# Masked cross attention of a two-layer decoder: how heads, softmax sums and stacked operands travel through memory

## The reference

```python
def _L0_xattn_ref(target, source, target_mask, source_mask, Wq, bq, Wk, bk, Wv, bv):
    # SIZE = 256, HEADS = 16, HEAD_DIM = 16, NEG = 1e6; target = x and source = ctx, (b, 256, 512)
    q = jnp.einsum('oc,bct->bot', Wq, target) + bq[None, :, None]
    k = jnp.einsum('oc,bcs->bos', Wk, source) + bk[None, :, None]
    v = jnp.einsum('oc,bcs->bos', Wv, source) + bv[None, :, None]
    ...
    dot = jnp.einsum('bhdt,bhds->bhts', q, k) / math.sqrt(HEAD_DIM)
    mask = target_mask[:, :, :, None] * source_mask[:, :, None, :]
    dot = mask * dot - (1.0 - mask) * NEG
    amap = jax.nn.softmax(dot, axis=-1) * mask
    out = jnp.einsum('bhts,bhds->bhdt', amap, v)
    return out.reshape(b, HEADS * HEAD_DIM, t)
...
x = _layernorm(x + _L0_xattn_ref(x, ctx, mask, mask, Wq, bq, Wk, bk, Wv, bv))
```

## Time and profile before

| | |
|---|---|
| Three timed runs | 3818.95, 3791.48, 3818.0 us; median 3818.0 |
| The profiled execution, its own time | 3803.1 us |
| Its span, first to last instruction | 3801.3 us |
| The changed stage, in the span | about 453 to 1309 us |
| Busy over the whole span | PE 82%, DVE 44%, ACT 33%, POOL 14% |
| Mean granted TensorE clock | 0.909 of full speed |

### The profile page before, as it was taken

The page is one execution under the profiler, slowest core; times in us unless marked ns, Lnnn a source line. Parts: engine busy times, 40 slices in busy tenths (PEclk is TensorE's granted clock), DMA queues, the critical chain, the costliest instruction groups (busy, mean ns, idle before and its releaser), DMA issues. The chain is left out here.

```text
span 3801.3 us, 48719 instructions
## 1 busy us (share of the span) xinstructions
PE 3109.5 (82%) x16306; PEld 2055.6 (54%) x16339; DVE 1682.5 (44%) x3232; ACT 1257.8 (33%) x3220; POOL 546.1 (14%) x551
## 2 busy tenths in 40 slices
PE   6999647786766469999978888599999997799894
PEld 5666422222222157777755555488888886444441
DVE  5666534554545222211215666366666665211113
ACT  2333214444444311111104444355565553111110
POOL 1000200111110120000000000233333332300002
PEclk9999867877888689999989999799999998999997
DMA  1000174434444220000010000211121113500323
GB/s 67 12 22 22 53 133 81 93 79 87 92 93 72 68 82 23 12 12 12 12 47 12 22 22 17 100 40 45 46 81 63 45 33 114 226 0 33 121 88 108
DMA packets 123827, 227.30 MB, mean 60 GB/s; under 512 B 14392, under 2 KB 27192, under 8 KB 123664
## 3 DMA queue, kind: packets, MB, share of 16 engines
q1 hardware_dynamic: 107488, 186.54, 18.3%
q0 software_dynamic: 7664, 27.40, 2.1%
q10 hardware_dynamic: 8512, 11.20, 1.0%
HBM read 157.36 MB, written 63.01 MB: 58 GB/s over the span
## 5 line engine op out<-in xcount | busy, mean ns | idle before, releaser
L1261 DVE TENSOR_REDUCE x_minus_max<-banks 128x2 f32<-128x1024 f32 x256 | 308.8, 1220 | 266.7 <-PE banks L1325 261.4
L1206 ACT ACTIVATE x_probs<-banks 128x512 f32<-128x512 f32 x512 | 285.9, 595 | 283.6 <-PE banks L1343 223.4
L1343 PE MATMUL banks<-x_stacked_q,x_stacked_k 53*128 53x512 f32 x512 | 254.7, 560 | 106.0 <-ACT x_probs L1206 70.0
L1325 PE MATMUL banks<-x_stacked_k,x_stacked_q 51*128 51x512 f32 x512 | 204.1, 529 | 106.2 <-DVE x_minus_max L1261 79.4
L1343 PEld LDWEIGHTS banks<-x_stacked_q,x_stacked_k 53*128 53x128 f32 x512 | 100.7, 220 | 350.1 <-ACT x_probs L1206 178.4
L481 ACT ACTIVATE a_probs<-banks,a_minus_max 128x128 f32<-128x128 f32 (+1 forms) x512 | 209.0, 425 | 146.7 <-DVE a_minus_max L564 144.7
L1355 PE MATMUL banks<-x_probs,x_v 128*32 128x512 f32 x1024 | 174.5, 760 | 6.6 <-ACT x_probs L1206 6.6
L2142 ACT ACTIVATE x_probs<-banks,x_minus_max,x_rroot 128x256 f32<-128x256 f32 x256 | 143.1, 566 | 91.4 <-DVE x_minus_max L2253 91.4
L2078 POOL TENSOR_TENSOR x_probs<-x_probs,x_inverse 128x512 f32<-128x512 f32 x128 | 133.3, 1041 | 275.3 <-DVE x_inverse L2287 275.3
L564 DVE TENSOR_REDUCE a_minus_max<-banks 128x2 f32<-128x512 f32 (+1 forms) x192 | 131.8, 686 | 83.8 <-remote 55.7
L2812 DVE TENSOR_TENSOR m_h<-banks,m_silu 128x512 f32<-128x512 f32 x39 | 27.0, 691 | 318.1 <-PE banks L2928 165.2
(11 more groups left out here) (369 smaller groups left out, 7684.5 us busy)
## 6 DMA issues: line engine op xcount, KB each, us to landing
x_parts_dram<-x_parts SPq DMA_DIRECT2D x16, 1024.0 KB, 5.0
x_x<-x_after SPq DMA_DIRECT2D x24, 512.0 KB, 4.5
x_stacked_k<-x_parts_dram SPq DMA_DIRECT2D x48, 256.0 KB
x_stacked_q<-x_parts_dram SPq DMA_DIRECT2D x48, 256.0 KB
x_after<-a_z SPq DMA_DIRECT2D x16, 512.0 KB, 2.8
x_z<-x_after SPq DMA_DIRECT2D x16, 512.0 KB, 7.4
x_after<-x_z SPq DMA_DIRECT2D x16, 512.0 KB, 2.8
x_context<-in_ctxT SPq DMA_DIRECT2D x16, 512.0 KB, 5.5
```

Of the source, the lines that this page charges most:

```text
L1206: act.activation(probs[:, n % 8, :], psum[at.bank(f"exp{n}")], ACT.Exp, scale=SCALE)\
L1261: dve.tensor_reduce(minus_max[:, c % 2, h % 4:h % 4 + 2, t], at.pair(use), AX.X, ALU.max, negate=True)\
L1325: ins = pe.matmul(at.pair(use)[:, half, :], stacked[0][to][rows, h, t * P:(t + 1) * P].bitcast(F32R), stacked[1][to][rows, h, :].bitcast(F ...
L1343: ins = pe.matmul(psum[at.bank(use)], stacked[1][u][rows, h // 2, s * P:(s + 1) * P].bitcast(F32R), stacked[0][u][rows, h // 2, :].bitcast ...
```

## The change

- `parts_dram` is laid out as (q or k, element, part, half, feature, head, 512), which is the order of the stack: a read for 16 partitions takes one contiguous run for each. `write_parts` writes for q and k, each part and each chunk of 128 partitions one DMA of 256 KB, eight in all, whose destination is walked as heads (4), halves (2), features (16), 512.
- A copied bank of heads goes whole to `heads_dram` (`write_heads`, one DMA of 256 KB), and is read back after two copies (`read_heads`): the sums as [32, 128], and the heads, 128 rows, one DMA each. These stand ahead of `stack` and of the loads.
- `spread_inverse` leaves SyncE. ScalarE gets the steps `send` (write the inverse) and `spread` (read it over 128 partitions, one DMA), at slots 20 and 24 for n = 1 of the element before and 52 and 56 for n = 0.
- Slots: `inverse''` from 15 to 18, `inverse` from 48 to 50, `stats''` 0 from 4 to 6, `stats''` 1 from 36 to 40, `normalise''` from 42 to 46. Semaphores that served both n get one for each.

```diff
@@ -851,7 +851,8 @@
                 add((kind, (q - at) // 16 + 1))
             if q == at + 48:
                 add((kind + "'", 0))
-        for step, at in ((("stats''", 0), 4), (("inverse''", 1), 15), (("stats''", 1), 36), (("normalise''", 0), 42), (("inverse", 0), 48)):
+        for step, at in ((("stats''", 0), 6), (("inverse''", 1), 18), (("send''", 1), 20), (("spread''", 1), 24), (("stats''", 1), 40),
+                         (("normalise''", 0), 46), (("inverse", 0), 50), (("send", 0), 52), (("spread", 0), 56)):
             if q == at:
                 add(step)
         for n in range(UNITS_IN_TAIL):
@@ -942,9 +943,9 @@
         sums = sb("sums", [FOLD, 2, P])
         inverse = sb("inverse", [FOLD, 2, P])
         inverse_rows = sb("inverse_rows", [P, 2, POS])
-        parts_dram = nc.dram_tensor(f"{name}_parts_dram", (2, 2, 2, SIZE, POS), F32).ap()
+        parts_dram = nc.dram_tensor(f"{name}_parts_dram", (2, 2, 2, 2, CH, H // 2, POS), F32).ap()
         mask_dram = nc.dram_tensor(f"{name}_mask_parts_dram", (2, B, len(STACKED_PAIRS), POS), F32).ap()
-        sums_dram = nc.dram_tensor(f"{name}_sums_dram", (2, 2, H // 2, POS), F32).ap()
+        heads_dram = nc.dram_tensor(f"{name}_heads_dram", (2, 4, P, POS), F32).ap()
         inverse_dram = nc.dram_tensor(f"{name}_inverse_dram", (2, 2, H // 2, POS), F32).ap()
         constants_loaded = sem("constants_loaded")
         masks_loaded = sem("masks_loaded")
@@ -964,18 +965,18 @@
         shift_ready = [sem(f"shift_ready{k}") for k in range(2)]
         context_done = sem("context_done")
         heads_copied = sem("heads_copied")
-        heads_moved = [sem(f"heads_moved{k}") for k in range(2)]
-        sums_loaded = sem("sums_loaded")
+        heads_written = [sem(f"heads_written{k}") for k in range(2)]
+        heads_read = [sem(f"heads_read{n}") for n in range(2)]
+        sums_loaded = [sem(f"sums_loaded{n}") for n in range(2)]
         inverted = sem("inverted")
-        inverse_written = sem("inverse_written")
-        inverse_loaded = sem("inverse_loaded")
+        inverse_written = [sem(f"inverse_written{n}") for n in range(2)]
+        inverse_loaded = [sem(f"inverse_loaded{n}") for n in range(2)]
         combine_steps = sem("combine_steps")
         moved = sem("moved")
         rstd_ready = sem("rstd_ready")
         out_ready = sem("out_ready")
         NORM_STEPS = 5
         COMBINE_STEPS = 6
-        MOVES = 8 * 16
         CONSTANTS = 16 * 7
 
         class At:
@@ -1049,47 +1050,41 @@
 
                 for w in range(2):
                     sp.wait_ge(low_ready, b * 4 + (w + 1) * 2)
-                    sp.dma_start(parts_dram[w, u].rearrange("k (c p) s -> p k c s", p=P), parts[:, w]).then_inc(parts_written, 16)
+                    for k in range(2):
+                        for c in range(TT):
+                            heads_of = slice(c * H // 4, (c + 1) * H // 4)
+                            sp.dma_start(parts_dram[w, u, k, :, :, heads_of, :].rearrange("g d h s -> h g d s"), parts[:, w, k, c, :])\
+                                .then_inc(parts_written, 16)
 
             def stack(b, u):
 
 
-                sp.wait_ge(parts_written, b * 32 + 32)
+                sp.wait_ge(parts_written, b * 128 + 128)
                 for w in (1, 0):
                     for half in range(2):
                         for j, pair in enumerate(STACKED_PAIRS):
                             sp.dma_start(stacked[w][u][HALF * half + CH * j:HALF * half + CH * (j + 1)],
-                                         parts_dram[w, u, pair[w]].rearrange("(h g d) s -> g d h s", g=2, d=CH)[half])\
+                                         parts_dram[w, u, pair[w], half])\
                                 .then_inc(stacked_ready[w][u], 16)
                         sp.dma_start(stacked[w][u][HALF * half + STACKED_MASK:HALF * half + STACKED_MAX],
                                      mask_dram[w, b].unsqueeze(1).broadcast_to([len(STACKED_PAIRS), H // 2, POS]))\
                             .then_inc(stacked_ready[w][u], 16)
 
-            def move_heads(b, u, c):
-
-                n, half = c // 2, c % 2
+            def write_heads(b, u, c):
+
                 sp.wait_ge(heads_copied, b * 4 + (c + 1))
-                for i in range(4):
-                    sp.dma_start(sums_dram[u, n, 4 * half + i:4 * half + i + 1, :], heads_out[32 * i + CH:32 * i + CH + 1, half, :])\
-                        .then_inc(heads_moved[half], 16)
-                for i in range(4):
-                    sp.dma_start(heads[64 * half + CH * i:64 * half + CH * (i + 1), n, :], heads_out[32 * i:32 * i + CH, half, :])\
-                        .then_inc(heads_moved[half], 16)
-
-            def fold_sums(b, u, n):
-
-                for half in range(2):
-                    sp.wait_ge(heads_moved[half], (b * 2 + (n + 1)) * MOVES)
-                sp.dma_start(sums[:, n, :], sums_dram[u, n].rearrange("h (k f) -> (h k) f", f=P)).then_inc(sums_loaded, 16)
-
-            def spread_inverse(b, u, n):
-
-                sp.wait_ge(inverted, b * 2 + (n + 1))
-                sp.dma_start(inverse_dram[u, n].rearrange("h (k f) -> (h k) f", f=P), inverse[:, n, :]).then_inc(inverse_written, 16)
-                sp.wait_ge(inverse_written, (b * 2 + (n + 1)) * 16)
-                for h in range(H // 2):
-                    sp.dma_start(inverse_rows[CH * h:CH * (h + 1), n, :], inverse_dram[u, n, h].unsqueeze(0).broadcast_to([CH, POS]))\
-                        .then_inc(inverse_loaded, 16)
+                sp.dma_start(heads_dram[u, c], heads_out[:, c % 2, :]).then_inc(heads_written[c % 2], 16)
+
+            def read_heads(b, u, n):
+
+
+                for k in range(2):
+                    sp.wait_ge(heads_written[k], b * 32 + (n + 1) * 16)
+                if n == 0 and not (isinstance(b, int) and b == 0):
+                    sp.wait_ge(combine_steps, b * COMBINE_STEPS - COMBINE_STEPS // 2)
+                by_head = heads_dram[u, 2 * n:2 * n + 2].rearrange("c (i q) s -> (c i) q s", q=32)
+                sp.dma_start(sums[:, n, :], by_head[:, CH, :].rearrange("h (k f) -> h k f", f=P)).then_inc(sums_loaded[n], 16)
+                sp.dma_start(heads[:, n, :], by_head[:, 0:CH, :]).then_inc(heads_read[n], 16)
 
             load_inputs(0, 0)
             for key, w in (("q", w_q), ("k", w_k), ("v", w_v)):
@@ -1107,11 +1102,10 @@
                     sp.wait_ge(mask_written, 16 * 2 * len(STACKED_PAIRS))
                     sp.wait_ge(cleared, 4)
                 if prev:
-                    move_heads(b - 1, 1 - u, 3)
+                    write_heads(b - 1, 1 - u, 3)
+                    read_heads(b - 1, 1 - u, 1)
                 if following:
                     stack(b + 1, 1 - u)
-                if prev:
-                    fold_sums(b - 1, 1 - u, 1)
                 if own:
                     if not (isinstance(b, int) and b < 2):
                         sp.wait_ge(stored[u], at.in_turn * 16)
@@ -1119,17 +1113,14 @@
                 if own and second:
                     sp.wait_ge(v_ready, b * 2 + 2)
                     load_inputs(b + 2, u)
-                if prev:
-                    spread_inverse(b - 1, 1 - u, 1)
                 if own:
-                    move_heads(b, u, 0)
-                    move_heads(b, u, 1)
-                    fold_sums(b, u, 0)
+                    write_heads(b, u, 0)
+                    write_heads(b, u, 1)
+                    read_heads(b, u, 0)
                 if prev:
                     store(b - 1, 1 - u)
                 if own:
-                    spread_inverse(b, u, 0)
-                    move_heads(b, u, 2)
+                    write_heads(b, u, 2)
                 if second:
                     write_parts(b + 2, u)
 
@@ -1158,9 +1149,8 @@
             def combine(b, u, n, loads):
 
                 s = (b * 2 + n) * (COMBINE_STEPS // 2)
-                for half in range(2):
-                    pool.wait_ge(heads_moved[half], (b * 2 + (n + 1)) * MOVES)
-                pool.wait_ge(inverse_loaded, (b * 2 + (n + 1)) * 16 * (H // 2))
+                pool.wait_ge(heads_read[n], b * 16 + 16)
+                pool.wait_ge(inverse_loaded[n], b * 16 + 16)
                 pool.tensor_tensor(heads[:, n, :], heads[:, n, :], inverse_rows[:, n, :], ALU.mult).then_inc(combine_steps, 1)
                 pool.wait_ge(combine_steps, s + 1)
                 pool.wait_ge(z_loaded[u], loads * 32)
@@ -1228,11 +1218,20 @@
                             ins = act.activation(v[:, 1 - u, s, :, 0:CH], v_biased[:, n, s % 2, :].rearrange("p (h d) -> p h d", h=H),
                                                  ACT.Copy, scale=source_mask[:, b + 1, s:s + 1])
                         ins.then_inc(v_ready, 1)
+                    if kind in ("send", "send''"):
+                        owner, of = (b, u) if kind == "send" else (b - 1, 1 - u)
+                        act.wait_ge(inverted, owner * 2 + (n + 1))
```

(12 more changed lines are left out.)

## The result

| | median of the timed runs | ratio to before, 95% interval |
|---|---|---|
| before | 3805.3 us (3791.5 to 3819.0, 4 runs) | |
| after | 3893.7 us (3888.9 to 3899.5, 4 runs) | 1.0233 [1.0208, 1.0259] |

The change makes the kernel 2.3% slower. The forecast was 3841 us with 3885 as its upper end; the measurement lies 9 us beyond that. The profiled execution of after took 3893.0 us, against 3803.1 of before: 90 us more, and they lie in the places that the forecast named, but they are larger, and s6 gains little of what it was to gain.

A forecast was written before the change was run, and what follows sets the result against it. Taken to bound: VectorE waiting for the folded sums (152.7 us) and TensorE for the maxima (31.0), with the context next. Opening 15, s0 7, s1 to s5 40, s6 −21, tail −3: +38 on 3803, 3841 us; range 3755 to 3885.

The forecast's parts named there:

- s6: Sequence without input loads for its slot 24: 13.9 us from early sums, 5.6 from the maxima wait, 1.5 from clock: −21.
- The term of the opening: Before the first scores: the narrow parts' write delays the start of stacking from 484.02 to 499, +15 us.
- 8 us more each, +40: Sequences s1 to s5: 6 us from the late context at slot 24 plus 2 us of slower clock, +40 together.
- 6 us later than today: Slot 24 of s1 to s5: context lands 55.1 us into the sequence, where the projection now starts at 48.8.
- 22 + 2.2: Parts' write: 22 us over a quarter of the engines at 95 GB/s, plus a fixed 2.2 us to land.
- the rival D: Clock behind slot 24 stays low 16 us, not 6: 4.5 us more in each of six sequences, 3868 us; chance 0.20.
- The rival B: Eight parts' writes spread as widely as the two did: −11 us together, 3792 us; chance 0.13.
- s0: First sequence: stacking 9 us later, context landing at 583 where the projection starts at 576.88: +7 us.
- so they cost nothing: ScalarE's four new issues a sequence, half a us each, cost nothing because its exponentials fill 36.2 of 108.7 us.
- The tail: From the last copy to the combine: eight issues less on each of two legs save 3 us.
- C: Contiguous source lifts stack reads to 225 GB/s, with the narrow write: −36 us, 3767 us; chance 0.12.
- E: Both the wide write and the quick stack reads: −96 us, 3707 us; chance 0.08.

The follow-up runs named there:

- experiment 11: Kernel before with VectorE's reciprocal at slot 26 instead of 15, statistics at 40 and normalising at 46, inputs still behind the stack: 3801.6 us, ratio 0.9980.
- order in memory alone (3): Kernel before with only the new memory order of the parts: eight narrow writes, contiguous reads, all else as before: 3938.2 us, ratio 1.0349.
- before, inputs first (6): Kernel before with one edit, the inputs issued ahead of the stack while the sums stay behind it: 3801.1 us, ratio 0.9982.
- wide write (1): Kernel after, new memory order kept, parts written over all engines in eight transfers a matrix, each from 32 partitions: 3821.0 us, ratio 1.0044.
- old order (2): Kernel after with the parts' memory layout, write and reads as in before, all other parts of the change kept: 3814.1 us, ratio 1.0027.
- after, inverse on SyncE (12): Kernel after with the write and spreading of the inverse back on SyncE's queue, narrow writes and all else kept: 3908.8 us, ratio 1.0269.
- old order, inputs first (5): Kernel after with the parts' old memory order and the inputs issued ahead of the stack: 3731.7 us, ratio 0.9818.
- inverse on SyncE (8): Kernel after with the old memory order, inputs ahead of the stack, and the inverse's write and spreading back on SyncE's queue: 3702.6 us, ratio 0.9724.
- before, inputs first, late reciprocal (10): Kernel before with inputs ahead of the stack and VectorE's reciprocal at slot 30 instead of 15, statistics at 42, normalising at 47: 3720.5 us, ratio 0.9776.

## Why the prediction was wrong

The table gives means over s1 to s5: "to slot 25" is from the sequence's start to its exponential of slot 25, "rest" from there to the next sequence, and the clock is the mean of the five windows of the rest, as those shown in experiment 11. Each row is one execution.

| kernel | to slot 25 | rest | clock in the rest |
|---|---|---|---|
| before | 50.2 | 51.4 | 0.89 |
| order in memory alone (3) | 68.3 | 52.1 | 0.87 |
| before, inputs first (6) | 49.4 | 51.0 | 0.90 |
| after | 59.7 | 55.9 | 0.79 |
| wide write (1) | 49.1 | 56.7 | 0.78 |
| old order (2) | 49.9 | 56.1 | 0.79 |
| after, inverse on SyncE (12) | 60.5 | 55.6 | 0.76 |
| before, late reciprocal (11) | 46.1 | 58.6 | 0.74 |
| old order, inputs first (5) | 36.2 | 51.6 | 0.79 |
| inverse on SyncE (8) | 31.4 | 54.3 | 0.80 |
| before, inputs first, late reciprocal (10) | 31.0 | 57.7 | 0.80 |

In all rows but that of experiment 5 the rest holds 190 matmuls; there it holds 177 to 188, because exponentials and matmuls are interleaved otherwise, so that row compares only roughly.

- **The mechanism of the wait was right.** The write is narrow (102 GB/s; 95 was taken); the reads gain nothing; the sums' wait goes; slot 24 waits for the context; the reads' source isn't their limit. The term of the opening was +15 and came out as 558.9 − 543.4 = 15.5.
- **The step that failed is the sum for s1 to s5.** "8 us more each, +40" measured 14.1 each, +70. Of this, 9.5 lie ahead of slot 25 ("6 us later than today") and 4.5 behind it (the clock, of which I took 2). Both terms were too small. TensorE's idle time ahead of the first projection, some 20 us by the forecast, is 17 to 33.
- **Of the 9.5:** the write was set at "22 + 2.2", from 2.1 MB at 95 GB/s. Alone, in the opening, that is what it took: 474.08 to 498.51, 24.4 us. In a sequence it takes 26 to 28; other transfers move beside it there (the heads' writes, the rows of the inverse), which I think is the cause, but no run separates it. The stack started on average 9.2 us later than before, where I had 7.4. The first projection, which waits for the context, came 44.3 us after the start of the stack, where the context had landed after about 40 (a context takes 25.1 us from issue to landing in the median, 19.0 before). I had added 3 for that, the upper end that I gave, and it measured 4. Less the 4.7 us of slack that the context had before, this makes the projection 8.8 us late.
- **The clock.** I asked how long TensorE stays at its lower level after the restart at slot 24, and made the long case the rival D, with the sign "0.50 for over 10 us". That sign came in two of the five sequences. Windows behind the restart in s1 and s2, then in s3 and s5:

```profile
715.50:720.50 5.00, 4.88 (x9) 1.47 (x13) 0.00 (x0) 0.60 (x1) 0.00 (x0) 0.50 0.00 1
720.50:725.50 5.00, 3.77 (x17) 0.92 (x13) 2.70 (x3) 2.30 (x4) 0.00 (x0) 0.84 0.00 0
830.00:835.00 5.00, 4.84 (x11) 1.44 (x13) 0.00 (x0) 0.60 (x1) 0.00 (x0) 0.59 0.00 2
835.00:840.00 5.00, 3.75 (x19) 1.35 (x12) 3.11 (x3) 2.41 (x5) 0.00 (x0) 1.00 0.00 0
```
```profile
942.00:962.00 20.00, 18.91 (x45) 5.32 (x49) 5.34 (x6) 5.74 (x10) 0.04 (x1) 0.50 0.00 1
1174.00:1195.00 21.00, 19.83 (x49) 5.43 (x49) 6.17 (x6) 6.37 (x11) 0.00 (x0) 0.50 0.00 0
```

  s1, s2 and s4 recover within some 5 us and their rest takes 52 to 54 us; s3 and s5 stay at 0.50 for 20 us, and theirs takes 62.8 and 57.6. So D came true in part, and the forecast's "some 6 us after the restart", read from s2 of before, held for three sequences. The length of the stall doesn't decide it: it was 32.8 us ahead of s1's restart and 32.9 ahead of s5's. That isn't all, for the clock also falls again late in a sequence, here at the end of s2:

```profile
874.00:890.00 16.00, 14.60 (x53) 5.36 (x52) 7.64 (x7) 8.39 (x15) 3.81 (x3) 0.50 0.32 117
```

  The question should have been put to the whole rest of the sequence. In the table, the three kernels whose stall lies at the reciprocal, ahead of slots 17 to 23, have 0.87 to 0.90 in the rest and take 51 to 52 us; those whose stall lies at slot 24 have 0.74 to 0.79 and take 56 to 59. Experiment 11 moves three of VectorE's steps, and the stall with them, and nothing else. So in the mean of five sequences the move of the stall to slot 24 goes with 4.5 to 7 us more, and it is the clock and not more waiting: the 190 matmuls of the rest keep TensorE busy for 42.1 us in before, 47.3 in after and 50.0 in experiment 11. The scatter is wide (0.74 to 0.96 over s1 to s5 of before, 0.69 to 0.89 in after). Why the clock falls isn't settled. The kernels without a long stall (5, 8 and 10) have 0.79 and 0.80 there too, so it seems to be less the stall at slot 24 that lowers it than the one at the reciprocal that is followed by a high one; and s6 of experiment 6, with its stall at the reciprocal, has 0.79, which speaks against even that as a rule.
- **The rival B** (3792, the write as wide as before) was too low for the same reason, and experiment 2 is exactly that case: 3814. By the profiles its s1 to s5 are 22 us longer than in before, where B had 5, and its s6 4.4 us shorter, where B had 14.
- **s0** was +7 and measured +11.4 (97.4 for 86.0). Its projection starts 12 us later in the sequence, because its stack starts 13 us later in it, where I had 9 (563.63 for 535.12, of which 15.5 are the opening).
- **s6** was −21 and measured −4.4: 9.3 us less up to slot 25 and 4.9 more behind it. The gain at slots 16 to 20 came (18.2 to 3.9), and 3 of the 5.6 us for the maxima. The 1.5 us "from the warmer clock" came with the other sign: from slot 25 on, 40.3 us at a clock of 0.80 where before took 35.4 at 0.98. And I missed a wait: "so they cost nothing", of ScalarE's four new issues, counted the time of issuing, half a us each, but `spread` is also a wait in ScalarE's order, for the small write of the inverse, which was issued at 1259.04, while the late stack was being read:

```profile
1273.67 0.65 ACTq L1228 DMA_DIRECT2D x_inverse_rows<-x_inverse_dram  x1
1274.41 1.09 ACT L1196 ACTIVATE x_probs<-banks 128x512 f32<-128x512 f32 x2 [9.92 <-DMA x_inverse_dram<-x_inverse]
```

  That is 10 us in s6, and hidden by the wait for the context in s1 to s5. Experiment 12 shows that it wasn't to be had by moving the issue: without it, the maxima were late by as much.
- **The tail** was −3 and measured −3.5: from the last copy at 1380.58 to the combine at 1392.28 it is 11.7 us where the earlier trace rows has 15.2.
- **C and E** (quick reads) are refuted by 130 GB/s at a share of 0.99, and by experiments 2 and 5. The range was too narrow at its upper end because D, which I bounded by one mechanism, stood alone for all that the clock could cost, and because the errors of the five terms were combined as if they were independent. The opening, s0 and s1 to s5 hang on the same write, and the term of s1 to s5 repeats one error five times: it was off by 30 us, where I had allowed a term 5 to 15. (The terms given for C add up to −35 and those for E to −94, not −36 and −96; nothing hangs on it.)

Sum of what was measured: 15.5 (opening) + 11.4 (s0) + 70.3 (s1 to s5) − 4.4 (s6) + 0.9 (s7 to its last copy) − 3.5 (tail) = 90.2, against 90 between the two profiled executions. So the failed step is this: the context's lateness and the clock behind slot 24 were taken as 6 + 2 us a sequence and measured 9.5 + 4.5, and s6's gain of 21 us, which left out ScalarE's wait and had the clock the wrong way, was 4.4.

## What to carry to other kernels

When a store is reshaped, look at the leading dimension of both its ends before anything else: here 2.1 MB cost 5.5, 11, 21 and 41 us (worked out from 380, 193, 102 and 51 GB/s) by how the transfers were cut, and a contiguous source for the reads, the thing it was done for, was worth nothing that the times show. When a wait is removed, find what lands last behind it and move both in one step: early sums alone cost 9 us or nothing, early inputs alone gave nothing, and both together gave 74 us. Moving the asking to a later slot (experiment 10, 3720.5 us) did as well as the faster delivery of experiment 5 (3731.7) and nearly as well as the best kernel (3702.6). A wait for a transfer that is put into the order of a busy engine costs more than its issue: 29 us in all between experiments 5 and 8. And a price read from one sequence should be checked in the others: the clock's recovery took 5 us in some and 20 in others.
